# Score products of a local attention: from four heads over the whole of TensorE to two head pairs in its two row halves

## The reference, cut to what matters

```python
x = attn_layer(shift_tokens(x), Wqkv[i], q_scale[i], k_scale[i], Wo[i]) + x      # i in 0..5
x = ffn_layer(shift_tokens(x), ln_g[i], ln_b[i], W1[i], b1[i], W2[i], b2[i]) + x
# inside attn_layer, 16 heads, window 32:
q, k = rotary(l2norm(q) * qs), rotary(l2norm(k) * ksc)
bk2, bv2 = look(bk), look(bv)                      # the window before, and this one: 64 keys
mask = (it < jb) | (it > jb + w) | (jb == -1)
sim = jnp.einsum('bhwie,bhwje->bhwij', bq, bk2) * QK_SCALE
sim = jnp.where(mask, -jnp.finfo(sim.dtype).max, sim)
attn = jax.nn.softmax(sim, -1)
out = jnp.einsum('bhwij,bhwje->bhwie', attn, bv2)
```

## Time and profile before

| | |
|---|---|
| median of 3 runs | 5802.88 us (5799.05 to 5819.71) |
| the profiled execution | 5801.78 us |
| its span, first to last instruction | 5800.0 us |
| PE busy | 4979.5 us, 86% |
| DVE busy | 4089.1 us, 71% |
| granted TensorE clock over the span | 0.929 of full speed |
| L1074 on PE | 774.5 us busy |

### The profile page before, as it was taken

The page is one execution under the profiler, slowest core; times in us unless marked ns, Lnnn a source line. Parts: engine busy times, 40 slices in busy tenths (PEclk is TensorE's granted clock), DMA queues, the critical chain, the costliest instruction groups (busy, mean ns, idle before and its releaser), DMA issues. The chain is left out here.

```text
span 5800.0 us, 90682 instructions
## 1 busy us (share of the span) xinstructions
PE 4979.5 (86%) x33904; PEld 2765.5 (48%) x34096; DVE 4089.1 (71%) x5868; ACT 2198.8 (38%) x2794; POOL 2000.6 (34%) x1547
## 2 busy tenths in 40 slices
PE   5999688898998999998898998998898998478886
PEld 2222255555555555555555555555555554222223
DVE  4677377777777777777777777777777776366652
ACT  0666333333333333333333333333333332035564
POOL 1111144444444444444444444444444442111110
PEclk6999799999999999999999999999999999579997
DMA  2222111112211122111222112112121111122210
GB/s 58 49 47 44 55 46 48 46 46 61 55 46 49 48 58 58 45 47 47 63 49 49 46 48 69 45 48 50 43 58 48 45 49 47 43 45 45 43 26 16
DMA packets 181029, 279.66 MB, mean 48 GB/s; under 512 B 58032, under 2 KB 79792, under 8 KB 174896
## 3 DMA queue, kind: packets, MB, share of 16 engines
q1 hardware_dynamic: 180880, 277.66, 19.5%
HBM read 61.70 MB, written 17.56 MB: 14 GB/s over the span
## 5 line engine op out<-in xcount | busy, mean ns | idle before, releaser
L792 POOL TENSOR_TENSOR l_u<-l_t 128x512 f32<-128x512 f32 x384 | 486.9, 1268 | 2110.3 <-DVE l_t L890 2110.3
L890 DVE SCALAR_TENSOR_TENSOR l_t<-l_r,l_qkvec,l_tab 128x1024 f32<-128x1024 f32 x768 | 949.3, 1278 | 294.5 <-ACT l_sq L821 291.3
L470 DVE TENSOR_REDUCE a_nmax<-a_pair 128x2 f32<-128x1024 f32 x512 | 612.4, 1221 | 374.5 <-PE a_pair L550 372.5
L1074 PE MATMUL l_r<-l_kbd,l_qn 128*32 128x256 f32 x12288 | 774.5, 390 | 44.5 <-DMA l_kbd<-l_kn 11.3
L388 ACT ACTIVATE a_pt<-a_st 128x512 f32<-128x512 f32 x1024 | 579.8, 597 | 335.4 <-PE a_st L534 325.3
L1021 PE MATMUL l_r<-xs,l_wqkv 128*128 (+1 forms) x768 | 431.9, 690 | 222.4 <-DVEq L956 189.0
L1074 PEld LDWEIGHTS l_r<-l_kbd,l_qn 128*32 128x32 f32 x12288 | 422.9, 111 | 302.2 <-issue 152.8
L1112 PE MATMUL l_r<-l_pbd,l_va 128*64 128x160 f32 (+1 forms) x6144 | 443.4, 297 | 127.7 <-DMA l_pbd<-l_pt 127.7
L534 PE MATMUL a_st<-a_qs,a_ks 75*128 75x512 bf16 x1024 | 391.7, 398 | 146.0 <-ACT a_pt L388 75.5
L801 POOL TENSOR_TENSOR l_p<-l_p,l_srec 128x1024 f32<-128x1024 f32 x192 | 365.3, 1903 | 415.6 <-DVE l_srec L961 284.7
L1112 PEld LDWEIGHTS l_r<-l_pbd,l_va 128*64 128x64 f32 x6144 | 400.2, 138 | 193.1 <-DVEq L896 108.3
(11 more groups left out here) (183 smaller groups left out, 7475.3 us busy)
## 6 DMA issues: line engine op xcount, KB each, us to landing
l_kbd<-l_kn SPq DMA_DIRECT2D x1536, 64.0 KB, 2.0
l_pbd<-l_pt SPq DMA_DIRECT2D x1344, 64.0 KB, 2.0
a_ks<-a_scr SPq DMA_DIRECT2D x96, 192.0 KB
a_qs<-a_scr SPq DMA_DIRECT2D x288, 64.0 KB
a_scr<-a_parts SPq DMA_DIRECT2D x48, 256.0 KB, 2.5
l_wqkv<-in_wqkv SPq DMA_DIRECT2D x6, 1536.0 KB, 6.9
l_pbd<-l_pt SPq DMA_DIRECT2D x192, 48.0 KB, 1.9
l_wo<-in_wo SPq DMA_DIRECT2D x6, 512.0 KB, 3.7
```

Of the source, the lines that this page charges most:

```text
L470: nc.vector.tensor_reduce(out=nmax[:, n, 2 * i:2 * i + 2], in_=pair[i][:], op=ALU.max, axis=AX.X, negate=True).then_inc(pair_dve[i], 1)
L792: nc.gpsimd.tensor_tensor(u[buf][:, 2 * a, :], t[:, 0, :], t[:, 3, :], ALU.subtract)
L890: last = nc.vector.scalar_tensor_tensor(out=t[:, 2 * half:2 * half + 2, :], in0=R[a][:, half, :].unsqueeze(1).to_broadcast([D, 2, T]), sca ...
L1074: last = nc.tensor.matmul(R[3][q:q + 32, bank, 256 * (w // 4):256 * (w // 4) + 256], qn[:, half, WIN * W:WIN * W + WIN], kbd[half][:, :, W ...
```

## The change: what it does

The four heads of a chunk become two pairs. A pair's q and k lie in 64 partitions, one row half of the array, and one product takes 64x32 weights and 2 x 64 = 128 columns. Each pair writes a PSUM bank of its own. There are 64 products in a chunk instead of 32, with half the rows and half the columns each; they go round the eight places (4 column groups, 2 row halves) one after another. `kbd` has two slots instead of four. Both masks stand ahead of all products. The units of the softmax come in another order, so the mask array, the last band piece and the columns that the value product reads follow it.

```diff
-        kbd = [sb(f"kbd{i}", [D, CH, KC]) for i in range(2)]
+        kbd = [sb(f"kbd{i}", [D, 2, KC]) for i in range(2)]
...
-                        sp.dma_start(band[96:128, NT, 0:(NT - 1) * CH * WIN],
-                                     turned[0:32, 0, CH:, :].rearrange("p u i -> p (u i)")).then_inc(pbd_full[c % 2], 16)
+                        sp.dma_start(band[96:128, NT, 0:(NT * CH - 2) * WIN],
+                                     turned[0:32, 0, 2:, :].rearrange("p u i -> p (u i)")).then_inc(pbd_full[c % 2], 16)
...
-                                sp.dma_start(kbd[i][q, r, WIN:KC], kn[q, i, :]).then_inc(S["kbd_full"], 16)
+                                sp.dma_start(kbd[i][q, r % 2, WIN:KC], kn[q, i, :]).then_inc(S["kbd_full"], 16)
...
                         for bank in range(2):
                             nc.tensor.matmul(R[3][:, bank, :], ident16[:], mask[:, bank, :], start=True, stop=False, skip_group_check=True)
-                            for w in range(8):
-                                W, q = 8 * bank + w, 32 * (w % 4)
-                                for half in range(2):
-                                    last = nc.tensor.matmul(R[3][q:q + 32, bank, 256 * (w // 4):256 * (w // 4) + 256],
-                                                            qn[:, half, WIN * W:WIN * W + WIN], kbd[half][:, :, WIN * W:WIN * W + 2 * WIN],
-                                                            start=False, stop=(half == 1), skip_group_check=True)
+                        for g in range(NT):
+                            for half in range(2):
+                                for w in range(4):
+                                    for pair in range(2):
+                                        W, heads = 4 * g + w, slice(64 * pair, 64 * pair + 64)
+                                        last = nc.tensor.matmul(R[3][32 * w:32 * w + 32, pair, 128 * g:128 * g + 128],
+                                                                qn[heads, half, WIN * W:WIN * W + WIN],
+                                                                kbd[half][heads, :, WIN * W:WIN * W + 2 * WIN],
+                                                                start=False, stop=(half == 1), skip_group_check=True)
                         last.then_inc(S["s_ready"], 1)
...
-                                    o = (g * CH + h) * WIN
+                                    o = ((bank * NT + g) * 2 + side) * WIN
...
-    tiles = [first] + [hidden] * (NT - 1)
-    a["mask"] = np.concatenate([np.tile(m, (1, CH)) for m in tiles], axis=1).astype(np.float32) * np.float32(MASKED)
+    tiles = ([first] + [hidden] * (NT - 1)) * 2
+    a["mask"] = np.concatenate([np.tile(m, (1, 2)) for m in tiles], axis=1).astype(np.float32) * np.float32(MASKED)
```

## The result

The changed kernel takes 5950.56 us (median of 4 runs, 5927.25 to 5965.96), the kernel before 5800.97 us (4 runs). The ratio is 1.0248, with a 95% interval of 1.0207 to 1.0289: slower by some 150 us. The profiled execution took 5965.96 us.

The account below looks back on a forecast made before the run. DVE was taken to set the pace in most stretches, PE in chunk 2 from the output products on. 5801.8 us - 20 + 14 = 5796, plus 1.1 for the median: 5797 us; range 5735 to 5900.

Parts of the forecast that it names:

- The block: Masks and score products of a chunk on PE: from 4.4 us to between 2.4 and 4.1 us, 0.3 to 2.0 shorter.
- The first rival: Score products: PE takes in records too slowly; about 6050 us at 45 ns a record, 6475 at 63 ns; chance 0.15.
- What of it reaches the end: Shorter scores gain nothing in chunks 0, 1 and 3; only chunk 2 of slow-clock bodies gains, 0.93 us each.
- Other edits at nothing: Larger last band piece (at most 0.1 us, covered), key transfers, DVE tiles, mask order and value-product columns: no cost.
- The debit: Longer PE idle time before the transposes drops the clock over chunk 2's output products in every fifth body: 14 us lost.
- The rival with the clock on the path: Slow L1011 after new idle time in half the bodies or all: 5820 to 5860 us, up to 5890; chance 0.13.
- The gain of 20 us: Chunk 2 of slow-clock bodies: transposes L1085 start 0.93 us earlier, 22 times, 20 us in all.
- The third rival: Clock falls less in the stack's bodies, 85.7 us each instead of 86.8: 53 us gained, 5750 us; chance 0.17.

Follow-up runs that it names:

- narrow products in turn: Kernel before with each 256-column score product cut into two of 128 on all rows, each next product going to the next column group: 5849.51 us, ratio 1.0106.
- half of the products: Changed kernel with the second half of each head's dimensions left out of the scores, 32 products a chunk instead of 64: 5794.12 us, ratio 0.9996.
- The copies: Changed kernel with 32 instead of 64 score products a chunk, plus one unused 128 KB copy a chunk issued by ACT: 5882.7 us, ratio 1.0167.
- both remedies: Changed kernel with PE's loop turned by one chunk and unread bf16 products filling PE's idle time: 5789.04 us, ratio 0.9991.

## Why the prediction was wrong

The time lies outside the range and on the other side of no change.

- **The block** was right, and at its lower end: 2.4 us, all eight places side by side. A record takes 16 ns. The first rival, records taken in too slowly, did not occur, though it was the only slower case that the prediction priced beyond the range. (Its price for 45 ns forgets the 0.15 us of room in chunk 2, some 7 us of 6050.) The estimate by the Trainium skill, "TensorE: Matmul & The Clock Gate", Part 1, of 25 ns from start to start is not borne out: 128 records with 128 weight loads ran in 2.03 us. The warning of the Trainium skill, "TensorEngine Tiling (Array Packing)", Instruction Overhead, against a tiling factor from a dimension that is already small, did not matter either: with 128 columns left the block took 2.4 us.
- **What of it reaches the end**: right. DVE waited for scores 2 times, and with the code short the time is that of before (0.9996). The count of places was off: L1088 waits for ACT 191 times, in all four chunks (2.44 us in chunk 3 of the body above), where the prediction let it wait in three.
- **Other edits at nothing** is the step that failed. It counted transfers, tiles and columns, and put the 512 instructions that the body's code gains at nothing without naming them. The first rival even named 256 instead of 128 per block, but asked only whether the array could take them in. The part that it left out: about 60 us for the loop that no longer fits, seen alone in the narrow products in turn, and the late bands that come with it. The windows say the same from the other side: 8.6 us gained in six bodies without transfers, 167 us lost in 37 bodies with them.
- **The debit** was of the right kind and too small. I took 14 us, with ends at 0 and 77, for falls over L1011. They were there in 11 of 48 bodies, 1.7 us each, about 19 us, so that item was near. Alone the falls are nothing net (half of the products: clock 0.884, no loss). What the prediction lacked is their meeting with late bands: the changed kernel lost 150 us and the longer loop alone 60, so some 90 us come from the short block and the longer loop together. The copies imitate this (1.7%). The sentence "A fall over L1112 in chunks 0 and 1 is covered by the wait behind it" (L1115 in the changed kernel) holds with bands in time, and it fails when they are 1 us late: 1 us and 2 us of slower products are more than the wait. How the 90 us divide among such chunks, slow products behind them and the jump is not shown.
- **The rival with the clock on the path** was the nearest case, up to 5890 us, and its sign in the profile, a clock under 0.91, was there. Its mechanism was there only in part: L1011 slow in 11 bodies, not in half or all. L1021 waiting for DVE as often as before was wrong: 21 times instead of 94.
- **The gain of 20 us** in chunk 2 can't be seen by itself in any run. Its count was near: in the kernel before 25 of the 48 chunks 2 don't wait for ACT, where the prediction took 22.
- **The third rival**, the clock falling less, was worth what was said (53 us at most), but it takes other edits to get it: 0.93% by filling idle time, 0.87% by extra traffic. In the first layer, where no transfers come in, a little of it is there (87.2 us a body instead of 88.6).

What stays open: where exactly the limit of the loop lies between 256 and 512 more instructions, and why the first layer's loop, with the same code, shows no transfers in the changed kernel, but does with some 60 instructions more. That the instruction transfers are what delays the bands rests on their coming together in the trace (4.36 us of issues without a packet, 5.16 with one) and on the imitation by copies; the transfers themselves were not moved. Why 51 us remain with both remedies, against the kernel before with one, was not looked into.

## What to carry to other kernels

Count the instructions of a loop's body on each engine before splitting products: what fits cost nothing here (up to 256 more), and past a limit every pass paid at the jump and in DMA traffic. The packets of the instruction queue in the profile tell which side of it a kernel is on. A change that makes PE idle where it is not the bound isn't free if its clock can fall into what follows; fill the idle time with products that nobody reads, or look how much cover stands behind. Try such a remedy on the kernel before as well, or its gain is taken for a part of the change's loss. In a packed array, send neighbouring instructions to different tiles.

## What the runs showed of the hardware

- Eight tiles of 64 rows and 32 columns worked side by side in fp32: 128 records in 2.03 us, 16 ns from one to the next, weight loads included.
- Eight records in a row for one column group take away much of the overlap of the groups: 4.33 us instead of 1.96 for the same 64 records. Four in a row don't: 1.97 us for 32 records of twice the columns.
- In the bodies whose instructions came in again PE waited 2.9 us at the jump back (29 waits, 85.1 us); with the loop turned so that it lies in another wait, 71 us of 150 came back.
- A packet of instructions that comes in while SP issues a band makes the issues take 5.16 us instead of 4.36, on average of 144 chunks.
- PE's loop of the later layers brought in some 8 packets a body at 1708 instructions a body (298 in 37 bodies), and 47 in 37 bodies at 1196; that of the first layer none at 1708 and 53 in six passes at 1768.
- The kernel before became 0.9% faster with 128 KB of useless copies a chunk; its idle time fell into other pieces and the granted clock was 0.936 instead of 0.929.
